# Merging two products into one matmul whose result lies over two PSUM banks

## The chip, the cores and the metric

The kernel runs on one core of a Trainium2 chip. The time is that of one execution on the device, in microseconds (us); the number that counts is the median of several runs. The engines are TensorE (PE, with its weight loads shown apart as PEld), VectorE (DVE), ScalarE (ACT), GpSimd (POOL) and SyncE (SP), which issues the DMAs.

## What is computed

A block of three residual steps on x of 8 x 256 tokens, 256 wide: half of a mixture of 8 experts, a gated delta-rule attention, and half of the mixture of experts again. The change lies in the attention:

```python
q, k, v = silu(causal_conv(x @ W_qkvz))      # 16 heads of q and k, 32 of v, 128 wide
q, k = l2norm(q) * 128 ** -0.5, l2norm(k)
def step(state, inp):                         # one step per token, in each head
    qt, kt, vt, gt, bt = inp
    state = state * jnp.exp(gt)[..., None, None]
    pred = jnp.einsum('bhk,bhkv->bhv', kt, state)
    delta = (vt - pred) * bt[..., None]
    state = state + kt[..., None] * delta[..., None, :]
    return state, jnp.einsum('bhk,bhkv->bhv', qt, state)
core = core * rsqrt(mean(core * core) + EPS) * norm_weight * silu(z)
return core.reshape(Bb, Ss, VAL_DIM) @ W_out
```

The kernel does not walk token by token. It cuts each sequence into chunks of 128 tokens and needs for each chunk the 128 x 128 products of k with k and of k with q, weighted by a decay.

## The kernel before

The attention's work is cut into 64 units: 16 heads of k times 4 pairs of sequences. A unit has four chunks of 128 tokens (t = 0 to 3) and two heads of v. Each engine walks through a list of steps in an order written out by hand, once per pass; in a pass every step works on another unit, given by `STAGE` (`products` and `mix` on the unit 11 ahead of the pass number, `output` and `join` on the one before it). There are three orders per engine: FILL for the first 11 passes, where only the front of the pipeline has work, then the steady order, then DRAIN. All steps are synchronised by semaphores, and an engine that waits holds up everything behind it in its list.

The steps around the change:

- `proj_qk`, `conv_qk`, `gate_qk` (PE; ACT then DVE; ACT) make q and k of a unit, transposed, in `qk`. `turn` (L1303, PE) turns them back, so that ACT can sum squares (L1499), POOL can work out scales (`scales`, `diag`) and DVE can make the decay by a scan (L1614).
- `products` (L1314, PE): four matmuls of k with k into bank `gen[2]`, and four of k with q into bank `gen[0]`, 128 columns each.
- `mix` (L1623, DVE): mix 0 multiplies the k-with-k bank by the decay into `mt_made`, mix 1 the k-with-q bank into `pt_made`. `spill` (SP) writes both to memory; ACT's `conv_qk` (L1465) two units later waits for that.
- `solve` (L1389, PE) writes `gen[0]`, which `weigh` (L1539, ACT) copies out. `on_state` 0 (L1409) and `output` 1 (L1421) write `gen[2]`; `join` (L1770, DVE) reads it. `output` 0 writes `gen[1]`.
- `z` (L1292), `proj_v` (L1280) and `project` (L1445) write the two `proj_bank`s. `add` (L1785, DVE) waits for `project`. `turns` (L1324, PE) waits for `gate_v` (L1482, ACT), which waits for `conv_v` (L1591, DVE).
- `blocks` (DVE) inverts small blocks for a whole head in pieces; which pieces a pass has depends on its number modulo 4, so there are four kinds of pass.

Before a matmul overwrites a bank, PE waits for whoever reads it: `bank0_read` for `gen[0]`, `bank2_read` for `gen[2]`. The steady orders, from the middle of the pass on:

```python
PE_ORDER = (..., ("project", 0), ("turn", 0), ("project", 1), ("proj_v", 2), ("proj_v", 3), ("solve", 1),
            ("inv_last",), ("products", 0), ("products", 1), ("z", 0), ("turns", 0), ("z", 1), ("turns", 1),
            ("output", 0), ("output", 1))
DVE_ORDER = (..., ("add", 0), ("from_state",), ("add", 1), ("blocks", 2), ("blocks", 3), ("conv_v", 2),
             ("conv_v", 3), ("scan",), ("mix", 0), ("mix", 1), ("shape",), ("join",))
```

Of the kernel before, what the change touches and what calls it, by code (L numbers as in the profile page):

```python
# [12 lines left out]
P = 128  # L13
# [15 lines left out]
HV = NV // NK  # L29
BP = BATCH // 2  # L30
UNITS = NK * BP
Q4 = 4
# [14 lines left out]
def at_least(eng, semaphore, value):  # L47

    if isinstance(value, int) and value <= 0:
        return  # L50
    eng.wait_ge(semaphore, value)
# [617 lines left out]
def build(nc, x_in, W_qkvz, W_ba, conv_weight, A_log, dt_bias, norm_weight, W_out, gate_w, w1, w2, w3, out,  # L669
          parts=("ffn", "attention", "ffn")):  # L670
    ctx = ExitStack()
    with ctx:
        Pools.program = ctx
        r = Pools(nc, ctx)
        x = r.sb("x", [P, NT, D])
        xnT = r.sb("xnT", [P, KD, T])
        c = {name: r.sb(name, shape, dtype) for name, shape, dtype in (
            ("ident", [P, P], F32), ("eps_p", [P, Q4], F32), ("ones", [P, P], F32), ("le", [P, P], F32),
            ("lt", [P, P], F32), ("gt", [P, P], F32), ("minus_half", [P, NT], F32), ("half", [P, NT], F32), ("minus_one", [P, NT], F32),
            ("zeros", [P, D], F32), ("iota_i", [P, TILES + 1], I32), ("iota", [P, TILES + 1], F32))}  # L680
        for name in ("x_loaded", "constants_made", "out_stored"):
            c[name] = r.dma_sem(name)
        c["experts_loaded"] = {f"f{n}_": [r.dma_sem(f"f{n}_experts_loaded{k}") for k in range(2)] for n in range(2)}
        rows_in = nc.dram_tensor("rows_in", (T, D), F32, kind="Internal").ap()
        sums = nc.dram_tensor("sums", (T + P, D), F32, kind="Internal").ap()
        build_constants(nc, c, x_in, x)
        n = 0
        pending = None
        for part in parts:
            if part == "ffn":  # L690
                build_ffn(nc, c, x, xnT, gate_w, w1, w2, w3, rows_in, sums, f"f{n}_", n == 0)
                pending = sums
                n += 1
            else:
                build_attention(nc, c, x, xnT, pending, W_qkvz, W_ba, conv_weight, A_log, dt_bias, norm_weight, W_out)
                pending = None
            Pools.end_part(nc)
        build_out(nc, c, sums, out)


def attention_front(nc, c, x, xnT, pending, tab, W_ba, A_log, dt_bias, steps_kept, steps_stored, begin_loads):

    ctx = ExitStack()
    with ctx:
# [30 lines left out]
        with nc.Block() as block:  # L735
# [92 lines left out]
            def _(dve):  # L828
# [61 lines left out]
                for h in range(HV):  # L890
# [33 lines left out]
FILL_SP_ORDER = (("blocks_out",), ("load_wo",), ("load_t",), ("load_vz",), ("load_steps",), ("blocks_in",),  # L924
                 ("load_d",), ("load_qk",), ("load_c",), ("spill",))
FILL_PE_ORDER = (("proj_qk", 0), ("proj_qk", 1), ("state",), ("project", 0), ("on_state", 0), ("proj_v", 2),
                 ("project", 1), ("z", 0), ("on_state", 1), ("products", 0), ("y_turn", 0), ("turn", 1), ("inv_n",),
                 ("inv_x", 32), ("solve", 0), ("y_turn", 1), ("proj_v", 3), ("turns", 0), ("inv_last",),
                 ("output", 0), ("turn", 0), ("inv_x", 64), ("solve", 1), ("z", 1), ("products", 1), ("output", 1),
                 ("turns", 1))  # L930
FILL_ACT_ORDER = (("conv_v", 2), ("turn_copies", 0), ("turn_copies", 1), ("lift",), ("weigh", 0), ("z_gate", 0),
                  ("z_gate", 1), ("turn", 1), ("turn", 0), ("inv_n",), ("conv_v", 3), ("conv_qk", 0), ("gate_v", 2),
# [38 lines left out]
def build_attention(nc, c, x, xnT, pending, W_qkvz, W_ba, conv_weight, A_log, dt_bias, norm_weight, W_out):  # L971

    ctx = ExitStack()
    with ctx:
        r = Pools(nc, ctx, "at_")
# [39 lines left out]
        qk = [r.sb(f"qk{k}", [P, 2, UT]) for k in range(2)]  # L1015
# [29 lines left out]
        half_way = r.sb("half_way", [P, 256])  # L1045
        up_turned = r.sb("up_turned", [P, 16, 16])

        bank = [r.ps(f"bank{k}", [P, 512]) for k in range(8)]
        proj_bank, inv_bank, gen = bank[0:2], bank[2:4], bank[4:8]

        def dram(name, shape):
            return nc.dram_tensor(name, shape, F32, kind="Internal").ap()
# [7 lines left out]
        names = ("w_out_ready", "nw_ready", "qk_projected", "v_projected", "z_projected", "qk_free", "v_free", "z_free",  # L1060
                 "acc_qk", "acc_v", "step_qk", "step_v", "qk_ready", "v_gated",
                 "ss_done", "scales_step", "vscale_ready", "b_ready",
                 "kscale_ready", "diag_ready", "decay_ready", "kk_done", "kq_done", "mt_ready",
                 "pt_ready", "v_turned", "qk_turned", "v_ready", "k_ready", "block_step", "low_ready", 
                 "inv_zeroed", "w_up_ready",
                 "x_psum", "x_ready", "n_psum", "n_copied", "n_copied_t", "last_psum", "invT_ready",
# [3 lines left out]
        s = {n: r.sem(n) for n in names}  # L1070
# [6 lines left out]
        def two(u):  # L1077

            return u[1] % 2

        def idx(u):
            return BP * u[0] + u[1]

        def of_two(u):

            return 2 * u[0] + u[1] // 2 + 1

        def shift(u, by):
            t = u[1] + by
            return u[0] + t // BP, t % BP  # L1090

        def seen(u, at, of):

            return min(max(idx(u) - STAGE[at[0]] + STAGE[of[0]] + (BEFORE[of] < BEFORE[at]), 0), UNITS)

        def channels(u, ct):

            return qk[two(u)][:, ct, :] if ct < 2 else vT[:, ct - 2, :]
# [29 lines left out]
        with nc.Block() as block:  # L1128
# [100 lines left out]
            def _(pe):  # L1229
                te = nc.tensor  # L1230

                def bank0_read(u, me):

                    at_least(pe, s["w_ready"], 2 * seen(u, me, ("solve", 0)) - 1)
                    at_least(pe, s["w_ready"], 2 * seen(u, me, ("solve", 1)))
                    at_least(pe, s["pt_ready"], seen(u, me, ("products", 1)))

                def bank1_read(u, me):
# [7 lines left out]
                def bank2_read(u, me):  # L1246

                    at_least(pe, s["mt_ready"], seen(u, me, ("products", 0)))
                    at_least(pe, s["rhs_ready"], seen(u, me, ("on_state", 0)))
                    at_least(pe, s["joined"], seen(u, me, ("output", 1)))  # L1250

# [51 lines left out]
                        last = te.transpose(gen[1 if a else 3][:, tt], qk[two(u)][:, a, tt], c["ident"][:])  # L1303
                    last.then_inc(s["qk_turned"], 1)

                def products(u, of):

                    me = ("products", of)
                    pe.wait_ge(s["qk_ready"], 2 * idx(u) + 2)
                    (bank0_read if of else bank2_read)(u, me)  # L1310
                    q, k = qk[two(u)][:, 0, :], qk[two(u)][:, 1, :]
                    for t in range(Q4):
                        tt = slice(P * t, P * t + P)
                        last = te.matmul(gen[0 if of else 2][:, tt], k[:, tt], q[:, tt] if of else k[:, tt], start=True, stop=True)  # L1314
                    last.then_inc(s["kq_done" if of else "kk_done"], 1)

                def turns(u, half):

# [59 lines left out]
                def solve(u, ch):  # L1378

                    if ch == 0:  # L1380
                        pe.wait_ge(s["invT_ready"], idx(u) + 1)
                        pe.wait_ge(s["v_ready"], 2 * idx(u) + 2)
                    else:
                        pe.wait_ge(s["rhs_ready"], idx(u) + 1)
                    bank0_read(u, ("solve", ch))
                    for b in range(2):
                        for v in range(HV):
                            n, m = 4 * b + 2 * ch + v, 2 * b + v
                            last = te.matmul(gen[0][:, P * m:P * m + P], invT[idx(u) % 3][:, n, :], vr[two(u)][:, n, :],  # L1389
                                             start=True, stop=True)  # L1390
                    last.then_inc(s["u_psum"], 1)
# [12 lines left out]
                def on_state(u, of):  # L1404

                    pe.wait_ge(s["s_ready"], idx(u) + 1)
                    (bank3_read if of else bank2_read)(u, ("on_state", of))
                    for b in range(2):
                        last = te.matmul(gen[2 + of][:, 256 * b:256 * b + 256], late_qk[two(u)][:, 1 - of, b, :],  # L1409
                                         state[:, 2 * b:2 * b + 2, :].rearrange("p n m -> p (n m)"), start=True, stop=True)  # L1410
                    last.then_inc(s["qs0_psum" if of else "ks0_psum"], 1)
# [44 lines left out]
            def _(act):  # L1456
                sc = nc.scalar

                def conv_qk(u, ct):

                    act.wait_ge(s["qk_projected"], 2 * idx(u) + ct + 1)

                    at_least(act, s["kq_done"], idx(u) - 1)
                    at_least(act, s["spilled"][two(u)], SPILL * (of_two(u) - 1))
                    sc.activation(channels(u, ct), proj_bank[ct][:], ACT.Copy, scale=taps_qk[u[0] % 2][:, ct, 3:4]).then_inc(s["acc_qk"], 1)  # L1465

# [116 lines left out]
            def _(dve):  # L1583
# [33 lines left out]
                def mix(u, of):  # L1617

                    dve.wait_ge(s["decay_ready"], idx(u) + 1)
                    dve.wait_ge(s["kq_done" if of else "kk_done"], idx(u) + 1)  # L1620
                    at_least(dve, s["spilled"][1 - two(u)], SPILL * of_two(shift(u, -1)))
                    both = gen[0 if of else 2][:].rearrange("p (t m) -> p t m", m=P).unsqueeze(2).to_broadcast([P, Q4, HV, P])
                    v_.tensor_tensor((pt_made if of else mt_made)[:].rearrange("p (t v) m -> p t v m", v=HV), both,  # L1623
                                     decay[:].rearrange("p (t v) m -> p t v m", v=HV),
                                     ALU.mult).then_inc(s["pt_ready" if of else "mt_ready"], 1)
# [291 lines left out]
```

## Time and profile before

| what | value |
|---|---|
| median of 3 runs | 2988.08 us (2986.07 to 2988.18) |
| profiled execution, its own time | 2983.82 us |
| its span, first to last instruction | 2982.1 us |
| mean granted TensorE clock | 0.949 |
| busy: PE, PEld, DVE, ACT, POOL | 2694.6, 1993.3, 1928.0, 1383.2, 689.3 us |
| records of L1314 (products) | 1024, median 275 ns |
| mix 0 and mix 1 (L1623) | 64 each, median 1225 and 1215 ns |

A busy time is the time in which an engine has an instruction in work. Matmuls overlap and their ends are modelled, so the starts of PE's records tell more than their lengths. An fp32 matmul stands as two records. The attention's passes lie between about 550 and 2480 us; the experts lie before and behind.

### The profile page before, as it was taken

The page shows a single profiled execution, that of the slowest core. Times are in us where ns is not written, and L with a number is a line of the kernel's source. Part 1 is how long each engine was busy: PE and PEld are TensorE (multiplying, and loading weights), DVE is VectorE, ACT ScalarE, POOL GpSimd, SP SyncE. Part 2 cuts the span into 40 slices and gives each one's busy share as a digit, 9 for nine tenths or more (in the row PEclk, how much of TensorE's full clock was granted, in tenths as well). Part 3 has the DMA queues.
Part 4 walks back from the last instruction along what each step waited for, and adds up shares of the span by engine and source line. Part 5 has one row for each costly group of instructions (what it writes and reads, how often), then busy time and mean ns, then how long its engine had stood idle before and what let it go on. Part 6 is the DMA issues. An engine that isn't in the chain of part 4 may idle for free. (4 is left out here: it accounts for less than half of the span.)

```text
span 2982.1 us, 58371 instructions
## 1 busy us (share of the span) xinstructions
PE 2694.6 (90%) x19346; PEld 1993.3 (67%) x19347; DVE 1928.0 (65%) x3648; ACT 1383.2 (46%) x4441; POOL 689.3 (23%) x956
## 2 busy tenths in 40 slices
PE   4999995555999999999999999999999994799996
PEld 4566664333677777777777777777777774566664
DVE  5122222578999999999999999999977544322221
ACT  0111111333766666666666666666665551111111
POOL 0222221222232232222232222232221111122221
PEclk7999997777999999999999999999999996799998
DMA  4223312245645545545545645645553313132322
GB/s 160 51 73 102 98 28 51 74 148 153 198 148 176 174 147 174 177 147 170 180 147 167 184 147 163 187 147 161 184 138 98 99 54 124 27 98 64 100 62 46
DMA packets 378125, 374.75 MB, mean 126 GB/s; under 512 B 213076, under 2 KB 293460, under 8 KB 377876
## 3 DMA queue, kind: packets, MB, share of 16 engines
q1 hardware_dynamic: 362900, 351.05, 37.7%
q0 software_dynamic: 14976, 20.46, 4.2%
q8 instruction: 147, 2.41, 0.3%
q14 instruction: 102, 0.84, 0.1%
HBM read 234.83 MB, written 138.67 MB: 125 GB/s over the span
## 5 line engine op out<-in xcount | busy, mean ns | idle before, releaser
L533 PE MATMUL f_ps_up<-f_wbuf,f_xgT 128*128 x1248 | 499.3, 544 | 5.4 <-issue 3.4
L628 DVE TENSOR_TENSOR f_h<-f_h,f_ps_up 128x448 f32<-128x448 f32 x156 | 96.9, 621 | 471.3 <-ACT f_h L602 471.3
L602 ACT ACTIVATE f_h<-f_ps_up 128x448 f32<-128x448 f32 x156 | 84.8, 543 | 635.3 <-PE f_ps_up L533 635.3
L533 PEld LDWEIGHTS f_ps_up<-f_wbuf,f_xgT 128*128 128x128 f32 x1248 | 231.2, 192 | 189.4 <-issue 184.9
L1591 DVE SCALAR_TENSOR_TENSOR at_qk<-at_bank,at_taps_qk,at_qk 128x510 f32<-128x510 f32 (+2 forms) x384 | 282.1, 745 | 67.4 <-ACT at_qk L1465 58.3
L1267 PE MATMUL at_bank<-xnT,at_w_qk 128*128 128x512 f32 x512 | 271.0, 658 | 58.3 <-DVE at_qk L1591 54.9
L1591 DVE SCALAR_TENSOR_TENSOR at_vT<-at_bank,at_taps_v,at_vT 128x510 f32<-128x510 f32 (+2 forms) x384 | 280.5, 744 | 35.8 <-ACT at_vT L1472 26.7
L1857 POOL TENSOR_SCALAR at_small<-at_small 128x4 f32<-128x4 f32 x64 | 17.7, 277 | 1144.8 <-ACT at_squares L1499 1144.8
L500 POOL DMA_INDIRECT sums<-f_y,f_row_of x78 | 123.9, 1588 | 582.2 <-DVE f_y L639 582.2
L555 PE MATMUL f_ps_y<-f_wbuf,f_hT 128*128 x1092 | 248.8, 379 | 1.6 <-DVE f_hT L632 1.6
L1292 PE MATMUL at_bank<-at_w_vz,xnT 128*128 128x256 f32 x1024 | 243.8, 381 | 7.1 <-DVE at_vT L1591 6.9
L1445 PE MATMUL at_bank<-at_w_out,at_yT 128*128 128x256 f32 x1024 | 242.6, 382 | 2.1 <-issue 1.6
L1280 PE MATMUL at_bank<-xnT,at_w_vz 128*128 128x512 f32 x512 | 231.5, 593 | 3.9 <-DVE x L1785 2.0
L555 PEld LDWEIGHTS f_ps_y<-f_wbuf,f_hT 128*128 128x128 f32 x1092 | 201.5, 190 | 27.0 <-issue 2.8
L1445 PEld LDWEIGHTS at_bank<-at_w_out,at_yT 128*128 128x128 f32 x1024 | 186.6, 191 | 26.2 <-issue 4.8
L1292 PEld LDWEIGHTS at_bank<-at_w_vz,xnT 128*128 128x128 f32 x1024 | 184.6, 190 | 28.7 <-DVE at_vT L1591 8.8
L1267 PEld LDWEIGHTS at_bank<-xnT,at_w_qk 128*128 128x128 f32 x512 | 95.9, 207 | 146.4 <-issue 136.8
L1499 ACT ACTIVATE at_squares<-at_bank 128x128 f32<-128x128 f32 x512 | 134.3, 277 | 119.4 <-PE at_bank L1303 118.1
L1472 ACT ACTIVATE at_vT<-at_bank,at_taps_v 128x512 f32<-128x512 f32 x128 | 88.0, 688 | 183.8 <-PE at_bank L1280 183.8
L1280 PEld LDWEIGHTS at_bank<-xnT,at_w_vz 128*128 128x128 f32 x512 | 96.5, 190 | 100.7 <-issue 96.3
L1785 DVE TENSOR_TENSOR x<-x,at_bank 128x512 f32<-128x512 f32 x128 | 87.8, 686 | 97.8 <-PE at_bank L1445 97.4
L1568 ACT ACTIVATE at_junk<-at_y 128x128 f32<-128x128 f32 x512 | 150.5, 298 | 0.0
(233 smaller groups left out, 5609.7 us busy)
## 6 DMA issues: line engine op xcount, KB each, us to landing
f_wbuf<-in_L_ffn_w_dram SPq DMA_DIRECT2D x48, 896.0 KB, 6.9
at_steps_e<-steps_kept SPq DMA_DIRECT2D x64, 512.0 KB, 6.8
pt_kept<-at_pt_made SPq DMA_DIRECT2D x64, 512.0 KB, 2.7
mt_kept<-at_mt_made SPq DMA_DIRECT2D x64, 512.0 KB, 4.1
at_mt<-mt_kept SPq DMA_DIRECT2D x64, 512.0 KB, 4.0
at_pt<-pt_kept SPq DMA_DIRECT2D x64, 512.0 KB, 4.6
qk_kept<-at_qk SPq DMA_DIRECT2D x64, 256.0 KB, 2.9
ks_kept<-at_ks_made SPq DMA_DIRECT2D x64, 256.0 KB, 2.7
```

What stands on the lines that cost most here:

```text
L500: nc.gpsimd.indirect_dma_start(out=sums, out_offset=bass.IndirectOffsetOnAxis(ap=row_of[:, t:t + 1], axis=0), in_=y[t % RING][:], in_offse ...
L533: last = te.matmul(ps_up[hf][w][:, 0:MH], xgT[b][:, k, :], wbuf[:, bass.ds(off + (w * WSIZE + k * M + hf * MH), MH)], start=(k == 0), stop ...
L555: last = te.matmul(ps_y[:, 0:D], hT[b][:, j, :], wbuf[:, bass.ds(off + (2 * WSIZE + j * D), D)], start=(j == 0), stop=(j == MJ - 1))
L628: v.tensor_tensor(part, part, ps_up[hf][1][:, 0:MH], ALU.mult).then_inc(h_ready, 1)
L1267: last = te.matmul(proj_bank[ct][:], w_qk[u[0] % 2][:, k, ct * P:(ct + 1) * P], xnT[:, k, UT * u[1]:UT * u[1] + UT], start=(k == 0), stop= ...
L1280: last = te.matmul(proj_bank[v][:], w_vz[:, k, v * P:(v + 1) * P], xnT[:, k, UT * u[1]:UT * u[1] + UT], start=(k == 0), stop=(k == KD - 1))
L1292: last = te.matmul(proj_bank[half][:, 256 * t:256 * t + 256], xnT[:, k, bass.ds(UT * u[1] + P * (2 * half + t), P)], w_vz[:, k, 2 * P:4 * ...
L1445: last = te.matmul(proj_bank[half][:, 256 * t:256 * t + 256], yT[:, 2 * (2 * half + t) + v, :], w_out[u[0] % 2][:, v, :], start=(v == 0), ...
L1472: sc.activation(channels(u, ct), proj_bank[v][:], ACT.Copy, scale=taps_v[:, v, 3:4]).then_inc(s["acc_v"], 1)
L1499: last = sc.activation(squares[:, t, :], src[:, P * t:P * t + P], ACT.Square, accum_out=small[two(u)][:, 4 * a + t:4 * a + t + 1])
L1568: last = sc.activation(junk[:, n, :], y[two(u)][:, n, :], ACT.Square, accum_out=osum[two(u)][:, n:n + 1])
L1591: ins = v_.scalar_tensor_tensor(out=dst[:, :, back:], in0=src[:, :, 0:SEQ - back], scalar=taps[:, 3 - back:4 - back], in1=dst[:, :, back:] ...
```

## The change

The two products share their weights (k) and are merged: for each chunk one matmul whose moving operand is q and k side by side, 256 columns. Its result takes a quarter of a tile `pair` that spans two adjoining banks; chunks 0 and 1 fall into what is still called `gen[2]`, chunks 2 and 3 into `gen[0]`. So `products` 0 and 1 are now halves of the chunks and no longer the two kinds of product. Each mix reads its own columns from both banks, waits for both halves, and whoever writes one of the two banks waits for both mixes. In the FILL order of PE the two turns go ahead, and both products follow them. The steady and DRAIN orders are not touched.

```diff
-                 ("project", 1), ("z", 0), ("on_state", 1), ("products", 0), ("y_turn", 0), ("turn", 1), ("inv_n",),
+                 ("project", 1), ("z", 0), ("on_state", 1), ("turn", 1), ("y_turn", 0), ("turn", 0), ("products", 0), ("products", 1), ("inv_n",),
                  ("inv_x", 32), ("solve", 0), ("y_turn", 1), ("proj_v", 3), ("turns", 0), ("inv_last",),
-                 ("output", 0), ("turn", 0), ("inv_x", 64), ("solve", 1), ("z", 1), ("products", 1), ("output", 1),
+                 ("output", 0), ("inv_x", 64), ("solve", 1), ("z", 1), ("output", 1),
...
-        bank = [r.ps(f"bank{k}", [P, 512]) for k in range(8)]
-        proj_bank, inv_bank, gen = bank[0:2], bank[2:4], bank[4:8]
+        bank = [r.ps(f"bank{k}", [P, 512]) for k in range(6)]
+        pair = r.ps("pair", [P, 2 * 512])
+        proj_bank, inv_bank = bank[0:2], bank[2:4]
+        gen = [pair[:, 512:1024], bank[4], pair[:, 0:512], bank[5]]
...
                     at_least(pe, s["w_ready"], 2 * seen(u, me, ("solve", 1)))
+                    at_least(pe, s["mt_ready"], seen(u, me, ("products", 1)))
                     at_least(pe, s["pt_ready"], seen(u, me, ("products", 1)))
...
                     at_least(pe, s["mt_ready"], seen(u, me, ("products", 0)))
+                    at_least(pe, s["pt_ready"], seen(u, me, ("products", 0)))
                     at_least(pe, s["rhs_ready"], seen(u, me, ("on_state", 0)))
...
-                    (bank0_read if of else bank2_read)(u, me)
-                    q, k = qk[two(u)][:, 0, :], qk[two(u)][:, 1, :]
-                    for t in range(Q4):
+                    (bank0_read if half else bank2_read)(u, me)
+                    for t in (2 * half, 2 * half + 1):
                         tt = slice(P * t, P * t + P)
-                        last = te.matmul(gen[0 if of else 2][:, tt], k[:, tt], q[:, tt] if of else k[:, tt], start=True, stop=True)
-                    last.then_inc(s["kq_done" if of else "kk_done"], 1)
+                        last = te.matmul(pair[:, 256 * t:256 * t + 256], qk[two(u)][:, 1, tt], qk[two(u)][:, :, tt], start=True, stop=True)
+                    last.then_inc(s["kk_kq_done"], 1)
...
-                    at_least(act, s["kq_done"], idx(u) - 1)
+                    at_least(act, s["kk_kq_done"], 2 * (idx(u) - 1))
...
-                    dve.wait_ge(s["kq_done" if of else "kk_done"], idx(u) + 1)
+                    dve.wait_ge(s["kk_kq_done"], 2 * idx(u) + 2)
                     at_least(dve, s["spilled"][1 - two(u)], SPILL * of_two(shift(u, -1)))
-                    both = gen[0 if of else 2][:].rearrange("p (t m) -> p t m", m=P).unsqueeze(2).to_broadcast([P, Q4, HV, P])
+                    kq_kk = pair[:].rearrange("p (t a m) -> p t a m", a=2, m=P)
+                    both = kq_kk[:, :, 0 if of else 1, :].unsqueeze(2).to_broadcast([P, Q4, HV, P])
```

## Rows read from the trace of the kernel before

**Rows 1.** Stages, fill then steady: length, busy time (instructions) per engine, PEclk, DMA.

```profile
550.00:740.00 190.00, 112.41 (x488) 63.56 (x488) 145.49 (x218) 71.92 (x277) 58.44 (x101) 0.78 0.45 140
...
785.00:2200.00 1415.00, 1405.07 (x12618) 1093.96 (x12617) 1302.81 (x2340) 961.77 (x3259) 364.82 (x597) 1.00 0.54 166
```

**Rows 2.** The same view of two passes of the steady order.

```profile
1311.30:1339.02 27.72, 27.70 (x251) 21.53 (x250) 26.14 (x38) 18.91 (x64) 9.79 (x14) 1.00 0.57 152
1339.02:1367.18 28.16, 27.69 (x250) 21.52 (x249) 24.38 (x72) 18.90 (x64) 6.37 (x11) 1.00 0.61 197
```

**Rows 3.** PE's waits from 785 to 2200 us: in total, times, longest.

```profile
PE at_bank L1324 <- ACT at_vT L1482: 6.6, 13, 0.9
```

**Rows 4.** Timeline of PE in one pass: start, us, line, shape, records.

```profile
1331.55 1.05 PE L1389 MATMUL at_bank<-at_vr,at_invT 128*128 128x128 f32 x8
1332.44 2.17 PE L1314 MATMUL at_bank<-at_qk 128*128 128x128 f32 x16
1334.44 1.89 PE L1292 MATMUL at_bank<-at_w_vz,xnT 128*128 128x256 f32 x8
1336.36 0.66 PE L1324 MATMUL at_bank<-ident,at_vT 128*128 128x128 f32 x4
1336.85 1.89 PE L1292 MATMUL at_bank<-at_w_vz,xnT 128*128 128x256 f32 x8
1338.58 0.60 PE L1324 MATMUL at_bank<-ident,at_vT 128*128 128x128 f32 x4
1339.02 1.95 PE L1421 MATMUL at_bank<-at_wv,at_pt 128*128 128x128 f32 x16
```

**Rows 5.** Timeline of DVE in the same pass.

```profile
1328.32 0.69 DVE L1785 TENSOR_TENSOR x<-x,at_bank 128x512 f32<-128x512 f32 x1 [0.44 <-PE at_bank L1445]
...
1331.12 4.52 DVE L1591 SCALAR_TENSOR_TENSOR at_vT<-at_bank,at_taps_v,at_vT 128x510 f32<-128x510 f32 x6
...
1337.87 1.22 DVE L1623 TENSOR_TENSOR at_mt_made<-at_bank,at_decay 128x1024 f32<-128x1024 f32 x1
1339.02 1.21 DVE L1623 TENSOR_TENSOR at_pt_made<-at_bank,at_decay 128x1024 f32<-128x1024 f32 x1
...
1342.24 0.69 DVE L1770 TENSOR_TENSOR at_y<-at_bank,at_o_state 128x512 f32<-128x512 f32 x1
```

**Rows 6.** Timeline of ACT in the same pass: weigh 1 and gate_v 3.

```profile
1332.64 0.58 ACT L1539 COPY at_wv<-at_bank 128x512 f32<-128x512 f32 x1 [0.20 <-PE at_bank L1389]
...
1335.67 0.63 ACT L1482 ACTIVATE at_vT<-at_vT 128x512 f32<-128x512 f32 x1 [0.89 <-DVE at_vT L1591]
```

**Rows 7.** PE, narrow windows that cut groups: products 1, output 1 twice (second groups).

```profile
1333.47 1.02 PE L1314 MATMUL at_bank<-at_qk 128*128 128x128 f32 x7
...
1339.91 1.06 PE L1421 MATMUL at_bank<-at_wv,at_pt 128*128 128x128 f32 x8
...
1284.48 1.06 PE L1421 MATMUL at_bank<-at_wv,at_pt 128*128 128x128 f32 x8
```

**Rows 8.** Timeline of DVE, mix 1 of another pass.

```profile
1283.47 1.22 DVE L1623 TENSOR_TENSOR at_pt_made<-at_bank,at_decay 128x1024 f32<-128x1024 f32 x1
```

**Rows 9.** Timeline of DVE in the fill, one mix 0.

```profile
645.30 1.23 DVE L1623 TENSOR_TENSOR at_mt_made<-at_bank,at_decay 128x1024 f32<-128x1024 f32 x1
```

**Rows 10.** Timeline of PE in the fill: the first turns, and products 0 once.

```profile
561.39 1.04 PE L1303 MATMUL at_bank<-ident,at_qk 128*128 128x128 f32 x8
...
646.67 0.79 PE L1314 MATMUL at_bank<-at_qk 128*128 128x128 f32 x5 [1.56 <-DVE at_mt_made L1623]
```

**Rows 11.** Timeline of ACT in the fill: conv_qk of the first passes.

```profile
564.28 1.28 ACT L1465 ACTIVATE at_qk<-at_bank,at_taps_qk 128x512 f32<-128x512 f32 x2
...
578.75 1.26 ACT L1465 ACTIVATE at_qk<-at_bank,at_taps_qk 128x512 f32<-128x512 f32 x2 [1.56 <-DMA mt_kept<-at_mt_made]
```

**Rows 12.** Timeline of PE, y_turn 1 and project 0 of another kind of pass.

```profile
1379.66 0.60 PE L1429 MATMUL at_bank<-ident,at_y 128*128 128x128 f32 x4
1380.43 1.96 PE L1445 MATMUL at_bank<-at_w_out,at_yT 128*128 128x256 f32 x8 [0.17 <-issue]
```

More of the change, by code:

```diff
@@ L1062, in build_attention @@
                  "ss_done", "scales_step", "vscale_ready", "b_ready",
-                 "kscale_ready", "diag_ready", "decay_ready", "kk_done", "kq_done", "mt_ready",
+                 "kscale_ready", "diag_ready", "decay_ready", "kk_kq_done", "mt_ready",
                  "pt_ready", "v_turned", "qk_turned", "v_ready", "k_ready", "block_step", "low_ready",
@@ L1304, in turn, with products @@
                     last.then_inc(s["qk_turned"], 1)
-                def products(u, of):
-                    me = ("products", of)
+                def products(u, half):
+                    me = ("products", half)
                     pe.wait_ge(s["qk_ready"], 2 * idx(u) + 2)
-                    (bank0_read if of else bank2_read)(u, me)
-                    q, k = qk[two(u)][:, 0, :], qk[two(u)][:, 1, :]
-                    for t in range(Q4):
+                    (bank0_read if half else bank2_read)(u, me)
+                    for t in (2 * half, 2 * half + 1):
                         tt = slice(P * t, P * t + P)
-                        last = te.matmul(gen[0 if of else 2][:, tt], k[:, tt], q[:, tt] if of else k[:, tt], start=True, stop=True)
-                    last.then_inc(s["kq_done" if of else "kk_done"], 1)
+                        last = te.matmul(pair[:, 256 * t:256 * t + 256], qk[two(u)][:, 1, tt], qk[two(u)][:, :, tt], start=True, stop=True)
+                    last.then_inc(s["kk_kq_done"], 1)
                 def turns(u, half):
```

## The prediction

> **What bounds the kernel now.** I read the stages first. Between 785 and 2200 us the attention runs its steady order: 1415.0 us in which PE shows 1405.1 us of records and VectorE 1302.8 us, at the full granted clock (1.00, the 2.4 GHz level) [rows 1]. That is where all but a few products run, so there the change is won or lost. One pass of the order takes 27.72 to 28.16 us, with PE records in 27.7 us of it [rows 2]. A reader would stop there and say "PE bound, so fewer PE records are time won". The second view corrects that: ends of matmuls are modelled, so a short wait of PE is hidden inside its busy time, and the list of PE's waits still keeps 13 waits at L1324 (turns 0) for ScalarE's gate of v [rows 3].
>
> So I followed one pass by starts alone. Matmuls of 128 columns that wait for nothing start every 0.111 us (solve 1: 8 records from 1331.55 to 1332.44); those of 256 every 0.216 us (z 1: 8 from 1336.85 to 1338.58) [rows 4]. Each fp32 matmul stands as two records. By that measure z 0 (8 records from 1334.44) should hand over at 1336.17, yet turns 0 begins at 1336.36: it waits 0.19 us for gate_v 3, which ends at 1335.67 + 0.63 = 1336.30 [rows 4, 6]. That gate follows conv_v on VectorE. VectorE's own path through the pass has no hole: add 1 at 1328.32 (it waits for PE's project 1), blocks, conv_v at 1331.12, the scan, mix 0 at 1337.87, mix 1 at 1339.02, shape, join at 1342.24 [rows 5]. The pass is therefore a ring: PE from output to project 1, VectorE from add 1 to the mixes, and PE again from turns 0 and the outputs. Both engines look full; the handovers decide.
>
> **The products.** Now 16 records take from 1332.44 to 1334.44, 2.00 us [rows 4]. After, 8 records of 256 columns: 8 x 0.216 = 1.73 us, 0.27 less, if nothing waits. But the second group writes the bank that solve 1 has filled, and waits as before for weigh 1 on ScalarE, which ends at 1332.64 + 0.58 = 1333.22; PE resumes at 1333.47 [rows 6, 7]. The first half would end at 1332.44 + 4 x 0.216 = 1333.30, so that wait stays. The second half shrinks from 0.97 us (1333.47 to 1334.44) to some 0.87. The saving is 0.10 us, bounds 0 and 0.27. I count it as nothing: z 0 then ends 0.10 us sooner and turns 0 waits 0.29 us instead of 0.19, and the outputs behind have a still later condition (next). If that cover were gone, 0.10 us on 51 passes gives 5 us, 0.27 gives 14.
>
> The Trainium skill, in "TensorE: Matmul & The Clock Gate", section "Back-to-back issue gap", puts streams of weight load and matmul at about 81 ns for 128 columns and 131 ns for 512. Read linearly (my estimate, from that page) 256 columns would cost some 98 ns, and 16 x 81 - 8 x 98 = 0.51 us would be saved in a unit: 27 us faster over 51 passes, if PE sets the pace. The trace does not agree: 111 and 216 ns, so two narrow matmuls cost nearly what a wide one does [rows 4].
>
> **The mixes.** Mix 0 now needs both groups of products, which are over 3 us before it starts (1334.44 against 1337.87) [rows 4, 5]: nothing. Its operand has a stride of 256 and crosses two banks; no row shows that. Bounds: 0, because the count of elements stays, and 0.07 us a mix, the part by which two mixes overlap (1337.87 + 1.22 against 1339.02), as if an instruction's start were paid again at the bank's edge [rows 5]. I take 0. At 0.07 us it would add 2 x 0.07 x 51 = 7 us.
>
> **The new wait, which decides.** Mix 1 now reads k-with-q columns in the bank that used to hold only k-with-k. So everything that writes this bank waits for pt_ready too: products 0, on_state 0 and output 1. The first two come long after. Output 1 does not: in the pass shown it starts at 1339.91, while mix 1 ends at 1339.02 + 1.21 = 1340.23 [rows 5, 7], 0.32 us later. In one kind of pass of four the gap is smaller, 1284.48 against 1283.47 + 1.22 = 1284.69 [rows 7, 8], 0.21. Of the 51 outputs under the steady order 38 are of the first kind and 13 of the second.
>
> To the gap comes the price of being released: from the end of the releaser to the first record. Nearest rows: 0.14 us in the fill, where products 0 waits for mt (645.30 + 1.23 = 646.53 to 646.67) [rows 9, 10], and 0.25 us at products 1 after weigh 1 [rows 6, 7], which carries more conditions. After such a stop the group itself is 0.08 us longer (0.97 for 8 records against 0.89) [rows 4, 7]. So 0.22 to 0.33; output 1 will carry six conditions where products 1 has four and the fill case two, so I extend the line once more to 0.44 as the upper bound, and take 0.38. Output 1 then moves by 0.32 + 0.38 = 0.70 us, or 0.20 + 0.38 = 0.58.
>
> Who waits behind it: PE runs in order, so inv_x 32, solve 0, proj_qk, state, on_state, the projects all move. VectorE's join does not (output 1 ends before 1342.24, when shape lets join start) [rows 5], but add 0 and add 1 wait for PE's projects, and from add 1 the ring closes: VectorE is late by the same amount at the next mix 1. The delay adds up pass by pass, unless PE loses a wait on the way. It does in one kind of pass: project 0 starts at 1380.43 where y_turn's four records from 1379.66 end at 1380.10 [rows 12], because conv_qk on VectorE frees its bank late. That takes back 0.33 us and the 0.07 of restart, so 13 of the 38 moves count 0.30.
>
> Sum: 25 x 0.70 + 13 x 0.30 + 13 x 0.58 = 17.5 + 3.9 + 7.5 = 28.9 us.
>
> **The fill.** Turns now go ahead of products. In its first pass the turns start at 561.39 behind eight product records (8 x 0.111 = 0.89 us) and ScalarE's squares hold back conv_qk until 564.28; that becomes 0.89 us sooner [rows 10, 11]. In later passes conv_qk waits for the spilled mt instead (1.56 us at 578.75) [rows 11]; turns earlier by 0.9 us gain nothing, since PE is busy in only 112 of 190 us there [rows 1]. In all -0.9 us. The added waits of the fill's products fall into the same slack. No DMA is added or moved; spill, waiting for pt and mt, keeps its order.
>
> **Total**: +28.9 - 0.9 = +28.0 us. The profiled execution took 2983.82 us, so 3011.8; the median of the runs shown, 2988.08, lies 4.26 above it, so I forecast **3016 us**, 0.9% slower. With release at 0.22 the sum is 25 x 0.54 + 13 x 0.14 + 13 x 0.42 - 0.9 = 19.9 (3008); with 0.44 it is 25 x 0.76 + 13 x 0.36 + 13 x 0.64 - 0.9 = 31.1 (3019).
>
> **Rivals.**
> - *PE sets the pace and the saving counts* (faster). For it: 27.70 us of records in 27.72 [rows 2]. Against: the hidden 0.19 us at turns 0. It decides only if mix 1 ended some 0.7 us earlier against output 1, so that the wait were free. Price: -5 us with weigh 1 still in the way, -14 without: 2974 to 2983. Chance 0.08. With the spacing that the Trainium skill states there it would be 2961; the rows at 111 and 216 ns leave that 0.02 of those 0.08.
> - *The delay is swallowed on the way round* (same). Output 1 moves, but PE has waits like that at project 0 in every pass. Price: only the fill's -0.9, so 2987. The rows show such a wait in one kind of pass of four. Chance 0.08.
> - *The fill gains in each of its 10 passes*, because the scan waits for diag and diag for the turns: -8.9 instead of -0.9, so 3008. Against: conv_qk's wait for the DMA. Chance 0.09.
> - *The two-bank read is slower*, +7 us: 3023. Nothing in the rows speaks for it; nothing there has tried it. Chance 0.07.
> - The forecast: 0.68.
>
> **Range and chances.** 3008 to 3019 is the forecast's own. To hold 8 in 10 I widen it to 3002 (the fill's gain together with a cheap release gives 3000) and to 3024 (the two-bank price gives 3023). Three runs lie within 2.1 us and 0.2% is 6 us, about what a measurement here can tell from no change. Slower by more than that: 0.68 + 0.09 + 0.07 = 0.84; same 0.08; faster 0.08.
>
> **What would show it.** Right: 8 records at L1314's successor, 0.216 us apart, a stop before the second four; output 1 starting some 0.3 us after mix 1 ends, in every pass; turns 0 still waiting for the gate; passes of 28.2 to 28.9 us where they were 27.7 to 28.2; the mixes still 1.22 us. Wrong: output 1 following output 0 without a stop, or project 1 at the old distance from the output before it. A first scan earlier by 0.9 us would show the fill's term; a shorter period of the later fill passes would refute it.

## The result, and the profile after

| | before | after |
|---|---|---|
| median of 4 runs each | 2987.07 us (2981.3 to 2988.18) | 3014.73 us (3011.79 to 3016.43) |
| profiled execution, its own time | 2983.82 us | 3011.79 us |
| steady order, first to 51st output 1 | 1390.07 us | 1421.39 us |

The changed kernel is slower: ratio 1.0095, 95% interval 1.0081 to 1.0109. The forecast was 3016 us, in a range of 3002 to 3024. TensorE's mean granted clock hardly differs (0.949 before, 0.952 after), and the steady stage ran at 1.00 in both.

The windows of the changed kernel, fill, steady and then three passes one behind the other, each from output 1 to the next output 1. Columns: window, length, busy time and instructions of PE, PEld, DVE, ACT, POOL, granted clock, share and GB/s of DMA.

```profile
550.00:740.00 190.00, 107.58 (x430) 58.12 (x429) 147.91 (x219) 73.31 (x281) 55.02 (x97) 0.79 0.43 138
785.00:2200.00 1415.00, 1379.58 (x11944) 1050.03 (x11943) 1279.78 (x2305) 940.31 (x3189) 353.96 (x583) 1.00 0.52 162
...
1438.10:1466.56 28.46, 27.86 (x241) 21.18 (x241) 26.21 (x37) 18.91 (x65) 9.78 (x14) 1.00 0.60 166
1466.56:1495.46 28.90, 27.85 (x240) 21.17 (x241) 24.36 (x72) 18.90 (x65) 6.36 (x11) 1.00 0.51 173
1495.46:1523.57 28.11, 27.64 (x240) 21.21 (x241) 26.41 (x42) 18.88 (x65) 6.31 (x11) 1.00 0.50 159
```

Against [rows 1] the same 1415 us hold less work of every engine, not of PE alone: fewer passes fit in. Against [rows 2] PE's busy time now falls short of the pass by 0.6, 1.05 and 0.5 us. By starts the four kinds of pass take 28.46, 28.46, 28.91 and 28.11 us, where before they took 27.71, 27.71, 28.16 and 27.86: 2.50 us more in four passes.

PE's waits under the steady order (us in total, times, longest):

```profile
PE at_pair L1424 <- DVE at_pt_made L1627: 25.6, 50, 0.7
PE at_bank L1327 <- ACT at_vT L1485: 7.4, 13, 0.9
```

The second line is the one of [rows 3], L1327 now being turns. The first is new: output 1 waits for mix 1, 50 times. One pass shows it. First PE, from solve 1 through products, z 0, turns 0, z 1 and turns 1 to the two outputs:

```profile
1457.53 1.05 PE L1392 MATMUL at_pair<-at_vr,at_invT 128*128 128x128 f32 x8
1458.42 2.09 PE L1317 MATMUL at_pair<-at_qk 128*128 128x256 f32 x8
1460.35 1.89 PE L1296 MATMUL at_bank<-at_w_vz,xnT 128*128 128x256 f32 x8
1462.33 0.66 PE L1327 MATMUL at_bank<-ident,at_vT 128*128 128x128 f32 x4
1462.82 1.89 PE L1296 MATMUL at_bank<-at_w_vz,xnT 128*128 128x256 f32 x8
1464.55 0.60 PE L1327 MATMUL at_bank<-ident,at_vT 128*128 128x128 f32 x4
1464.99 1.06 PE L1424 MATMUL at_bank<-at_wv,at_pt 128*128 128x128 f32 x8
1466.56 1.13 PE L1424 MATMUL at_pair<-at_wv,at_pt 128*128 128x128 f32 x8 [0.51 <-DVE at_pt_made L1627]
```

Then DVE in the same pass:

```profile
1461.53 2.28 DVE L1617 TENSOR_TENSOR_SCAN at_decay<-at_steps_e,at_decay 128x1024 f32<-128x1024 f32 x1
1463.84 1.23 DVE L1627 TENSOR_TENSOR at_mt_made<-at_pair,at_decay 128x1024 f32<-128x1024 f32 x1
1464.98 1.21 DVE L1627 TENSOR_TENSOR at_pt_made<-at_pair,at_decay 128x1024 f32<-128x1024 f32 x1
1466.12 2.18 DVE L1781 SCALAR_TENSOR_TENSOR at_y<-at_y,at_osum,at_zs 128x128 f32<-128x128 f32 x8
```

And ACT: weigh 1, then the gate of v that turns 0 waits for:

```profile
1458.62 0.59 ACT L1542 COPY at_wv<-at_pair 128x512 f32<-128x512 f32 x1 [0.20 <-PE at_pair L1392]
...
1461.64 0.63 ACT L1485 ACTIVATE at_vT<-at_vT 128x512 f32<-128x512 f32 x1 [0.88 <-DVE at_vT L1594]
```

What the reader is to see. Mix 1 ends at 1464.98 + 1.21 = 1466.19 and output 1 begins at 1466.56, 0.36 us later by the unrounded times. Without the wait it would follow output 0 after eight records, at 1464.99 + 0.89 = 1465.88. In [rows 4, 7] output 1 began 0.32 us *ahead* of the end of mix 1. The products are shorter, 1.93 us (1458.42 to 1460.35) against 2.00, and nothing comes of it: z 0 would hand over at 1460.35 + 1.73 = 1462.08, but the gate ends at 1462.27 and turns 0 starts at 1462.33. That wait was 0.19 us and is now 0.25. The mixes last 1.23 and 1.21 us, as before.

That PE's delay reaches VectorE shows in VectorE's waits: `add` waits longer for PE's `project`, before the change and after it (800 to 2180 us; in total, times, longest):

```profile
DVE x L1785 <- PE at_bank L1445: 50.5, 72, 1.4
DVE x L1789 <- PE at_bank L1448: 63.3, 72, 1.3
```

By stages the two profiled executions differ so: ahead of the attention −3.6 us (first proj_qk at 546.43, before 550.01), from there to the first output 1 +3.4, steady order +31.3, drain to the last add −0.2, from the last add into the second experts −3.1 (to their first matmul with weights of an expert: 79.1 us, before 82.2). Together +27.9.

### The profile page after: what moved, and what is told of

Read it like the earlier page. It is cut to its first block and busy times, and to the rows that moved or that the text cites. A ratio compares the mean times of both kernels' runs of the same rounds, so it can differ in the third digit from the quotient of the medians.

```text
span 3010.0 us, 57475 instructions
## 1 busy us (share of the span) xinstructions
PE 2692.3 (89%) x18834; PEld 1963.5 (65%) x18835; DVE 1931.3 (64%) x3648; ACT 1382.9 (46%) x4441; POOL 687.0 (23%) x956
```

## Experiments

The theory: the whole loss is output 1's wait for mix 1, fed back through a ring of PE and VectorE; the merge itself is worth nothing. Rivals: the merged matmul or the read over two banks costs or gains something; the fill counts for more. Each kernel was timed in 5 rounds beside the kernel before on the same chip; a ratio is to that kernel, with its 95% interval in brackets. Passes are starts from output 1 to output 1, steady order is the first to the 51st output 1, both in the profiled execution.

### The wait alone

The kernel before, with nothing but the new condition in `bank2_read`. All else is as before: narrow products, two kinds of product in two banks, the old fill.

```diff
                     at_least(pe, s["mt_ready"], seen(u, me, ("products", 0)))
+                    at_least(pe, s["pt_ready"], seen(u, me, ("products", 1)))
                     at_least(pe, s["rhs_ready"], seen(u, me, ("on_state", 0)))
```

> The kernel before, with nothing changed but that whoever writes gen[2] also waits for mix 1 (pt_ready). Theory (the wait of output 1 is the whole price): output 1 starts 0.36 us after mix 1 ends instead of 0.32 or 0.20 before it, its group takes 0.08 us more, and project 0 takes back 0.40 in one pass of four. Passes of 28.46, 28.46, 28.91 and 28.11 us as in the changed kernel, some 31 us more over the steady order: about 3018 us, 1.010 to 1.011 of the kernel before. Rival (the wide matmuls or the read over two banks cost the time): within 3 us of the kernel before.

Measured: 3014.68 us (3011.4 to 3017.32) against 2984.87, ratio 1.0095 [1.0079, 1.0110]. Passes 28.46, 28.46, 28.91, 28.10; steady order 1421.15 us. One output 1 and its mix 1, in the timelines of PE and of DVE:

```profile
1470.36 1.13 PE L1422 MATMUL at_bank<-at_wv,at_pt 128*128 128x128 f32 x8 [0.51 <-DVE at_pt_made L1624]
```

```profile
1468.79 1.22 DVE L1624 TENSOR_TENSOR at_pt_made<-at_bank,at_decay 128x1024 f32<-128x1024 f32 x1
```

Again 0.35 us from 1468.79 + 1.22 to 1470.36. The time came out 3 us under the expected 3018, the passes as expected. One added condition makes the whole loss, pass by pass.

### The old order in the fill

The changed kernel with PE's FILL order of before.

```diff
-                 ("project", 1), ("z", 0), ("on_state", 1), ("turn", 1), ("y_turn", 0), ("turn", 0), ("products", 0), ("products", 1), ("inv_n",),
+                 ("project", 1), ("z", 0), ("on_state", 1), ("products", 0), ("y_turn", 0), ("turn", 1), ("inv_n",),
...
-                 ("output", 0), ("inv_x", 64), ("solve", 1), ("z", 1), ("output", 1),
+                 ("output", 0), ("turn", 0), ("inv_x", 64), ("solve", 1), ("z", 1), ("products", 1), ("output", 1),
```

> The changed kernel with PE's old FILL order. Theory (the fill's new order brings 0.9 us once, in the first pass): 0.9 us more than the changed kernel, 3015 to 3016 us, the first conv_qk of the second unit 0.9 us later after the first proj_qk. Rival (from the first proj_qk to the first output the changed kernel lost 3.4 us against the kernel before, and the new order is why): 3 us less than the changed kernel, about 3011 us.

Measured: 3016.51 us (3013.36 to 3018.52), ratio 1.0103 [1.0088, 1.0119]. That is 1.8 us above the changed kernel's median, with overlapping ranges: the time alone settles nothing. The term can be seen at its place. From conv_qk of the first unit to that of the second VectorE takes 10.92 us before and 10.90 here, 11.27 at most in a run with the old order; with the new order it is 10.47 in the changed kernel and 10.03 to 10.52 in the others. So the new order gives 0.4 to 0.9 us in the first pass. From that second conv_qk to the first output 1, however, the profiled runs spread from 221.1 to 224.7 us with the old order and from 222.6 to 226.6 with the new one. The rival, a gain in each of the fill's passes, would need 9 us less there and is not seen.

### The narrow matmuls in the merged layout

The changed kernel with two matmuls of 128 columns in place of each of 256; banks, waits and mixes are unchanged.

```diff
-                        last = te.matmul(pair[:, 256 * t:256 * t + 256], qk[two(u)][:, 1, tt], qk[two(u)][:, :, tt], start=True, stop=True)
+                        for c in range(2):
+                            at = 256 * t + P * c
+                            last = te.matmul(pair[:, at:at + P], qk[two(u)][:, 1, tt], qk[two(u)][:, c, tt], start=True, stop=True)
```

> The changed kernel with its banks, waits and orders, but eight matmuls of 128 columns in place of four of 256. Theory (what the wide matmuls save on PE only makes turns 0 and output 1 wait longer): within 2 us of the changed kernel, steady passes still of 28.46, 28.46, 28.91 and 28.11 us. Rival (the saving counts on the path): 0.10 to 0.27 us more in each of 51 passes, 5 to 14 us more, 3020 to 3029 us.

Measured: 3013.98 us (3013.3 to 3015.43), ratio 1.0097 [1.0082, 1.0113]. PE's timeline, products and z 0:

```profile
1459.10 2.12 PE L1319 MATMUL at_pair<-at_qk 128*128 128x128 f32 x16
1461.07 1.89 PE L1296 MATMUL at_bank<-at_w_vz,xnT 128*128 128x256 f32 x8
```

1.97 us against 1.93 with the wide ones, and the same time. Because the second half still waits for weigh 1, this run puts only 0.04 us a pass back, 2 us in all, and not the 0.10 to 0.27 that were expected of the rival; the total time could not show so little. The steady order can: 1421.72 us against 1421.39, 0.3 us more where 2 us would have come if PE's work set the pace. The merge of the matmuls is invisible.

### Output 1 moved behind the wait

The changed kernel with output 1 taken out of its place and put behind `inv_x` at the start of PE's next pass, so that mix 1 is over when it comes. Every condition is kept; the work is the same, in another order. The FILL and DRAIN orders follow.

```diff
-    "solve": -1, ... "output": -1,
+    "solve": -1, ... "output": -1, "output_late": -2,
...
-PE_ORDER = (("inv_x", 32), ("solve", 0), ...
+PE_ORDER = (("inv_x", 32), ("output_late",), ("solve", 0), ...
...
-            ("products", 1), ("z", 0), ("turns", 0), ("z", 1), ("turns", 1), ("output", 0), ("output", 1))
+            ("products", 1), ("z", 0), ("turns", 0), ("z", 1), ("turns", 1), ("output", 0))
```

> The changed kernel with output 1 moved behind the first step of PE's next pass (inv_x 32, some 0.6 us of PE work that waits for nothing), so that PE has work while mix 1 runs. Theory (the loss is PE standing idle at output 1): the stop vanishes or falls under 0.2 us, passes come back to 27.7 to 28.2 us, and the time to that of the kernel before within 4 us (2983 to 2991). Rival (mix 1 is late for others too, or join on VectorE now waits for output 1): passes stay above 28.2 us and the time above 3000 us.

Measured: 2983.51 us (2979.56 to 2985.24), ratio 0.9992 [0.9983, 1.0001]. Passes 27.71, 27.71, 28.16, 27.80; steady order 1388.75 us. PE's timeline, output 0 and the moved output 1 (between them lie the small matmuls of `inv_x`), and mix 1 on DVE:

```profile
1452.40 1.06 PE L1424 MATMUL at_bank<-at_wv,at_pt 128*128 128x128 f32 x8
...
1454.01 1.16 PE L1424 MATMUL at_pair<-at_wv,at_pt 128*128 128x128 f32 x8
```

```profile
1452.40 1.21 DVE L1627 TENSOR_TENSOR at_pt_made<-at_pair,at_decay 128x1024 f32<-128x1024 f32 x1
```

Mix 1 ends at 1453.61; output 1 comes at 1454.01, 0.12 us behind the last record of `inv_x` (1453.89), and the list of PE's waits under the steady order no longer holds it. The loss is gone, and only the loss: with the wait covered, the merged products bring nothing that can be measured.

### The same move on the kernel before

The edit is the one above, made on the kernel before the change:

```diff
-            ("products", 1), ("z", 0), ("turns", 0), ("z", 1), ("turns", 1), ("output", 0), ("output", 1))
+            ("products", 1), ("z", 0), ("turns", 0), ("z", 1), ("turns", 1), ("output", 0))
```

> The kernel before, with output 1 moved behind inv_x 32 of PE's next pass, as in the run of that order on the changed kernel (which took 2983.5 us). Theory (with the wait covered, what the wide matmuls save is hidden behind the wait of turns 0): within 2 us of that run and of the kernel before, passes of 27.71, 27.71, 28.16 and 27.8 us. Rival (the merge gains and the late order costs as much, or the other way round): 5 us or more off the kernel before.

Measured: 2983.59 us (2979.85 to 2988.08) against 2986.44, ratio 0.9993 [0.9984, 1.0002]; passes 27.71, 27.71, 28.16, 27.86; steady order 1389.13 us. The medians of the two late kernels differ by 0.1 us, as expected; the distance to the kernel before, 2.9 us, is 0.9 more than expected, with an interval that holds 1. The new place of output 1 is neutral by itself, so the kernel above did not hide a gain or a loss of the merge behind it: 1388.75 merged, 1389.13 not. Had PE's shorter products (0.07 us a pass) counted, that would be 3.5 us.

### Fewer conditions on the waiting step

The changed kernel, where output 1 waits, of all readers of its bank, for mix 1 alone (the other readers are over before mix 1 can start). Its conditions fall from six to three.

```diff
-                    (bank2_read if ch else bank1_read)(u, ("output", ch))
+                    if ch:
+                        at_least(pe, s["pt_ready"], seen(u, ("output", 1), ("products", 0)))
+                    else:
+                        bank1_read(u, ("output", 0))
```

> The changed kernel, but output 1 asks of the bank's readers for pt_ready alone; mix 0, from_state and join, for which it also asked, come before mix 1 on VectorE, so nothing else is left unguarded. Theory (the price of a release grows by some 0.055 us with each condition that output 1 carries, 0.14 us with two, 0.25 with four, 0.36 with six): with three conditions output 1 starts some 0.20 us after mix 1 ends instead of 0.36, 0.16 us less in each of 51 passes, 8 us less than the changed kernel, about 3006 us. Rival (the price is that of the release itself): the distance stays at 0.36 us and the time within 2 us of the changed kernel.

Measured: 3005.43 us (3001.03 to 3007.55) against 2986.44, ratio 1.0061 [1.0047, 1.0074]. Passes 28.25, 28.25, 28.70, 27.89; steady order 1410.16 us, 11.2 us under the changed kernel. Output 1 on PE and its mix 1 on DVE:

```profile
1350.67 1.13 PE L1427 MATMUL at_pair<-at_wv,at_pt 128*128 128x128 f32 x8 [0.30 <-DVE at_pt_made L1630]
```

```profile
1349.31 1.21 DVE L1630 TENSOR_TENSOR at_pt_made<-at_pair,at_decay 128x1024 f32<-128x1024 f32 x1
```

From 1349.31 + 1.21 = 1350.52 to 1350.67 is 0.15 us, where it was 0.36; 0.20 was expected. The conditions that were dropped had all been met long before; asking for them delayed the first matmul by 0.21 us, in each pass.

The number of conditions does not explain this by itself. In the changed kernel products 1 asks for five conditions where before it asked for four (bank `gen[0]` now waits for mix 0 too), and yet its second half starts no later after weigh 1 (1458.62 + 0.59 = 1459.21), 0.21 us instead of 0.25:

```profile
1459.41 1.10 PE L1317 MATMUL at_pair<-at_qk 128*128 128x256 f32 x4
```

And turns 0 asks for six, yet starts 0.06 us after the gate (1462.27 to 1462.33; before, 1336.30 to 1336.36). The trace holds what the views leave out: PE's own wait instructions, each for one or two conditions, and one more condition on the step's first weight load. At output 1 of the changed kernel the wait for mix 1 passes at 1466.24, and two more wait instructions follow, at 1466.34 and 1466.45, though all they ask for is long met; the weight load comes at 1466.53. Here the wait for mix 1 passes at 1350.56 and the weight load comes at 1350.64, with none between. Of 40 steady passes the 0.36 us holds in 35 and the 0.15 in all 40. At products 1 one wait instruction stands behind the one for weigh 1, in the kernel before and in the changed one. At turns 0 the condition on the gate sits on the weight load itself, and the other five were asked for some 2 us earlier. So the 0.21 us are two wait instructions, 0.106 us each, that stand behind the late one. Where PE gets through a wait before the late condition is met, as at turns 0, it adds nothing. No run changed the order of the conditions alone.

### Both outputs late

The changed kernel with both outputs in the next pass, around `solve` 0, so that z and turns can spread out. The FILL and DRAIN orders follow.

```diff
-PE_ORDER = (("inv_x", 32), ("solve", 0), ...
+PE_ORDER = (("inv_x", 32), ("output", 0), ("solve", 0), ("output", 1), ...
...
-            ("products", 1), ("z", 0), ("turns", 0), ("z", 1), ("turns", 1), ("output", 0), ("output", 1))
+            ("z", 0), ("products", 1), ("z", 1), ("turns", 0), ("turns", 1))
```

> The changed kernel with PE's steady order changed so that nothing stands where its releaser is late: z 0 between the two products (weigh 1 runs meanwhile), z 1 ahead of the turns (gate_v runs meanwhile), and both outputs in PE's next pass, output 0 behind inv_x 32 and output 1 behind solve 0 (mix 1 runs meanwhile). Theory (the ring of PE and VectorE sets the pace and the stops at products 1, turns 0 and output 1 are its only slack): the stops vanish, passes of 27.3 to 27.5 us, 0.2 to 0.5 us less than before the change in each, 10 to 25 us less than the kernel before, 2960 to 2975 us. Rival (VectorE or ScalarE sets the pace, or output 0 now waits for the copies of v): 2980 us or more.

Measured: 2989.01 us (2983.19 to 2991.83), ratio 1.0007 [0.9998, 1.0016]; passes 27.68, 27.68, 28.14 and 28.27. The expectation missed. Output 0 in PE's timeline, the copies of v in ACT's, and two lines of DVE's waits (800 to 2180 us):

```profile
1318.42 1.13 PE L1423 MATMUL at_bank<-at_wv,at_pt 128*128 128x128 f32 x8 [0.18 <-issue]
```

```profile
1317.22 0.84 ACT L1521 ACTIVATE at_vr<-at_bank,at_t_vscale 128x256 f32<-128x256 f32 x2 [2.23 <-PE at_bank L1326]
```

```profile
DVE x L1788 <- PE at_bank L1447: 37.8, 72, 1.3
DVE at_y L1773 <- PE at_pair L1423: 18.9, 49, 0.5
```

Output 0 now stands close behind the copies of v that its bank waits for. They end at 1317.22 + 0.84 = 1318.06, where the last record of `inv_x` starts too, and output 0 starts 0.36 us later; its first wait instruction, which asks for the copies, passes at 1318.10, and two more follow. Output 1 comes after it, and join, which in the changed kernel waited for nothing in this stretch, waits for it 49 times, 18.9 us in all, while `add`'s wait falls from 63.3 to 37.8. VectorE's side of the ring got the wait that PE's side lost.

### Both late, with fewer conditions

The kernel above, with output 0 asking only for the copies of v, `solve` 0 and output 1 only for mix 1.

```diff
-                    bank0_read(u, ("solve", ch))
+                    if ch:
+                        bank0_read(u, ("solve", ch))
+                    else:
+                        at_least(pe, s["pt_ready"], seen(u, ("solve", 0), ("products", 1)))
...
-                    (bank2_read if ch else bank1_read)(u, ("output", ch))
+                    if ch:
+                        at_least(pe, s["pt_ready"], seen(u, ("output", 1), ("products", 0)))
+                    else:
+                        at_least(pe, s["v_ready"], 2 * seen(u, ("output", 0), ("turns", 0)) - 1)
```

> The run with z 0 and z 1 moved and both outputs late, with the conditions that others imply taken off output 0 (the copies of v alone), solve 0 and output 1 (pt_ready alone). Theory (what was left there is the price of release, 0.34 us at output 0 and through it 0.37 us at join): the stop at output 0 falls by some 0.2 us, join no longer waits, passes of 27.4 to 27.5 us where they were 27.68 and under 28.0 where they were 28.26, 10 to 20 us less than that run, 2969 to 2979 us, faster than both kernels. Rival (the stop is not from the conditions, or another step takes its place): within 4 us of that run, 2985 to 2993 us.

Measured: 2981.17 us (2976.88 to 2983.42) against 2983.84, ratio 0.9989 [0.9980, 0.9998]. Passes 27.47, 27.47, 27.91 and 28.06; steady order 1383.0 us, 7.1 under the kernel before. Join's wait in DVE's waits:

```profile
DVE at_y L1779 <- PE at_pair L1429: 2.7, 12, 0.2
```

Output 0 starts 0.15 us after the last record of `inv_x` in place of 0.36 (1312.60 to 1312.75), with one wait instruction in place of three, and join's wait is nearly gone. The steady order is shorter, but the expectation missed: 2981 us lies above the 2969 to 2979 that were expected. The last kind of pass stayed above 28.0 us; in it PE stands before `project`, 13 times and 8.2 us in all, and the profile names no releaser. And from the second conv_qk to the first output 1 this run took 226.6 us, the longest of all, 5.5 more than the kernel before; whether its FILL order or chance made that, one profile does not tell. Its ratio is the lowest of the kernels here, 0.1% under the kernel before, which is less than the 0.2% that a measurement tells apart.

## Why the prediction was right

**The ring.** Right, and shown from both ends: the wait added to the old kernel makes the whole loss, and the wait covered in the new one takes it back. PE's busy share of nearly 100% in [rows 2] did not mean that PE set the pace. The rival that said so would have gained with wide against narrow matmuls, and with the late output in the merged kernel against the same move without the merge; the steady orders differ by 0.3 and 0.4 us where it asks for 2 and 3.5.

**The products.** Counted as nothing; the saving is 0.07 us (0.10 was expected) and turns 0 waits 0.06 us longer. Records of 256 columns follow each other every 0.216 us here too, although their moving operand now is two separate runs of 128 columns. By my estimate from the Trainium skill's spacing in "TensorE: Matmul & The Clock Gate", section "Back-to-back issue gap", 0.51 us a pass would have been saved; the trace does not agree, with 0.111 and 0.216 us a record. The estimate also took each record for a whole matmul, where an fp32 matmul stands as two.

**The mixes.** Counted as nothing; medians 1224 and 1212 ns against 1225 and 1215. The read over two banks costs nothing.

**The release.** The term that was mis-sized. I took 0.38 us for release and restart together, with 0.44 as the upper bound from a line through the conditions of three steps. It was 0.36 + 0.08 = 0.44, the bound itself. That the line met it was luck: the price does not go by the count of conditions. It was 0.14 us with two, 0.15 with three, 0.25 with four and 0.36 with six at output 1, but 0.21 with five at products 1 of the changed kernel, and 0.06 with six at turns 0, which [rows 4, 6] already showed (1336.30 to 1336.36). What the traces show to count are the wait instructions behind the late one: none in the fill's case and in the run with fewer conditions, one at products 1 before and after, two at output 1. With 0.44 the steady sum is 25 × 0.76 + 13 × 0.36 + 13 × 0.64 = 32.0; measured are 31.3, over the 50 steps from the first to the 51st output 1. With 0.38 it was 28.9.

**The delay that is swallowed.** As a rival it fell: three kinds of pass grew by 0.75 us, and one by 0.25. I had put the smaller gap (0.58) and the absorbing wait (0.30) into two kinds of pass; in the rows both show in one, and the other grows by the full 0.75. The sum is hardly touched: 2.50 us in four passes, where my terms at 0.44 give 0.76 + 0.76 + 0.36 + 0.64 = 2.52.

**The fill.** −0.9 us is there at its place, with 0.4 to 0.9, but later waits in the fill move by up to 4 us between runs of one order and hide it: from the first proj_qk to the first output 1 the four profiles with the old order took 236.2 to 240.0 us, the six with the new one 237.1 to 240.9. What makes them move, with the same order, stays open; conv_qk's wait for the spilled mt stands there before and after.

**The total.** +28.0 against +27.97 in the profiled runs is closer than its terms deserve, and that is luck. The steady order gave 2.4 us more than I had summed. Against that stand −3.6 us ahead of the attention and −3.1 behind it, in code that the change does not touch, and +3.4 in the fill. The last add to the second experts took 78.4 to 81.6 us in the experiments, so the 82.2 of before lies at the high end. The medians differ by 27.7 us, and they say the same without hanging on one execution.

## What to carry to other kernels

When two results move into one bank, list everyone who writes that bank next and ask which of them runs *before* the new reader ends; a gap of 0.32 us that nothing had enforced, and the price of release on top, cost 0.95% of the kernel. An engine that looks full may still be one half of a ring: compare the starts, and find the handover that ends last, before counting a saving on it. If a wait can't be avoided, put the step where the wait is already over, ask on it only for what the other conditions do not imply, and see how many wait instructions stand behind the one that is met last.

## What the runs showed of the hardware

The time from the end of a releaser to PE's first matmul hung on how many of PE's wait instructions stand behind the one that is met last, even where all they ask for is long met: 0.36 us with two (output 1 of the changed kernel) and 0.15 us with none (the run with fewer conditions), 0.106 us for each. By the medians that was worth 9.3 us of the total (3014.73 against 3005.43), by the steady orders 11.2. Where the late condition sat on the step's first weight load it was 0.06 us (turns 0). A step that stops once also runs its own group 0.07 to 0.08 us longer (1.13 against 1.06 us at output 1). A VectorE operation that reads across two adjoining PSUM banks costs no more than one that stays in one (1224 and 1212 ns against 1225 and 1215).
